# Two cross-attention and two feed-forward blocks on one core: low parts of the first weights and context tiles on DVE, statistics of x blocks 4 to 7 ahead of evacuations

## The reference

```
x = x + _L0_xattn_ref(_layernorm(x), ctx_4096, Wq, Wk, Wv, Wo)      # 16 heads of 96, 4 key-value heads; keys: context and x itself
x = x + _L0_ffn_ref(_layernorm(x), ...)                             # relu(x up)^2 down, plus a routed low-rank part, layernorm
x = x + _L1_xattn_ref(_layernorm(x), ctx_4096, Wq, bq, Wkv, bkv, Wo, bo)   # 32 heads of 128, 8 key-value heads
x = x + _L1_ffn_ref(_layernorm(x), W, b, A, Bmat, LiMEs)            # x W + b, plus a gated low-rank part
```

## Time and profile before

| | before |
|---|---|
| median of 3 runs | 1207.34 us (1207.11 to 1208.05) |
| the profiled execution | 1206.82 us |
| its span | 1205.0 us |
| PE busy | 1159.5 us (96%) |
| DVE busy | 556.8 us (46%) |
| ACT busy | 506.0 us (42%) |
| POOL busy | 371.0 us (31%) |

### The profile page before, as it was taken

One profiled execution on the slowest core, in us unless ns is written; L12 is line 12 of the kernel. 1 busy time (PEld: TensorE's weight loads), 2 busy tenths in 40 slices (PEclk: granted clock), 3 DMA queues, 4 the chain that ended last, 5 costly groups with the idle time before them and its releaser, 6 DMA issues.

```text
span 1205.0 us, 15331 instructions
## 1 busy us (share of the span) xinstructions
PE 1159.5 (96%) x5582; PEld 916.4 (76%) x5582; DVE 556.8 (46%) x1011; ACT 506.0 (42%) x1377; POOL 371.0 (31%) x249
## 2 busy tenths in 40 slices
PE   5999999999999999996999999999999999999998
PEld 3777777777777768874888888888888888888774
DVE  4355346246237753258552533435243352433654
ACT  4365256247246624233452624435253351623620
POOL 3043034024024255455440502405032240412440
PEclk9999999999999999998999999999999999999997
DMA  7010001000000031200110100102001020100001
GB/s 255 1 40 27 1 26 39 0 26 26 0 18 1 1 117 58 88 35 1 36 53 1 52 35 35 52 0 87 1 35 52 2 85 0 38 35 1 12 1 70
DMA packets 10325, 43.42 MB, mean 36 GB/s; under 512 B 1301, under 2 KB 1557, under 8 KB 7605
## 3 DMA queue, kind: packets, MB, share of 16 engines
q1 hardware_dynamic: 10292, 42.99, 10.2%
HBM read 40.89 MB, written 2.10 MB: 36 GB/s over the span
## 4 chain that ended last, share of the span: by engine, by line
PE 85%; DVE 6%; ACT 4%; issue 3%; POOL 2%; DMA 0%; DVEq 0%; ACTq 0%; POOLq 0%
PE work L433 15%; PE work L435 15%; PE work L434 15%; PE work L494 7%; PE yb L433 5%; PE yb L435 4%; PE yb L434 4%; PE pt L504 3%; PE ov L435 3%; PE ov L433 3%; PE ov L434 3%; PE pt L435 3%; PE pt L434 3%; PE pt L433 3%; ACT prob L919 1%
## 5 line engine op out<-in xcount | busy, mean ns | idle before, releaser
L1089 POOL TENSOR_TENSOR prob<-prob,exp_rcp 128x512 f32<-128x512 f32 (+1 forms) x96 | 127.3, 1327 | 626.8 <-DVE exp_rcp L1264 626.8
L433 PE MATMUL work<-xT_hi,q_hi 128*128 128x512 f32 (+1 forms) x448 | 181.5, 405 | 4.8 <-DVE xT_lo L1349 4.8
L919 ACT ACTIVATE prob<-work,neg_max 128x128 f32<-128x128 f32 (+1 forms) x384 | 149.6, 408 | 74.4 <-DVE neg_max L1287 73.0
L435 PE MATMUL work<-xT_hi,q_lo 128*128 128x512 f32 (+1 forms) x448 | 177.8, 397 | 0.0
L434 PE MATMUL work<-xT_lo,q_hi 128*128 128x512 f32 (+1 forms) x448 | 177.7, 397 | 0.0
L494 PE MATMUL work<-kT,qT 128*128 128x128 f32 (+1 forms) x768 | 128.2, 310 | 1.1 <-DVE qT L1201 0.9
L494 PEld LDWEIGHTS work<-kT,qT 128*128 128x128 f32 (+1 forms) x768 | 114.1, 191 | 14.4 <-issue 1.7
L871 ACT ACTIVATE pT_hi<-pt 128x512 fp32r<-128x512 f32 x128 | 73.9, 603 | 109.1 <-PE pt L504 109.1
L1317 DVE TENSOR_TENSOR oT_lo<-ov,oT_hi 32x128 fp32r<-32x128 f32 (+2 forms) x160 | 67.3, 421 | 102.9 <-ACT oT_hi L877 101.6
L433 PE MATMUL yb<-o_hi,oT_hi 128*128 128x512 f32 x224 | 93.9, 419 | 10.4 <-DVE oT_lo L1317 10.4
L433 PEld LDWEIGHTS work<-xT_hi,q_hi 128*128 128x128 f32 (+1 forms) x448 | 81.4, 182 | 26.8 <-DVE xT_lo L1349 5.3
(11 more groups left out here) (182 smaller groups left out, 2109.1 us busy)
## 6 DMA issues: line engine op xcount, KB each, us to landing
q_raw<-in_l_q SPq DMA_DIRECT2D x8, 1024.0 KB, 4.7
o_raw<-in_l_o SPq DMA_DIRECT2D x8, 1024.0 KB, 4.7
kv_raw<-in_l_kv SPq DMA_DIRECT2D x8, 515.0 KB, 3.3
q_raw<-in_l_q SPq DMA_DIRECT2D x4, 768.0 KB, 4.3
o_raw<-in_l_o SPq DMA_DIRECT2D x4, 768.0 KB, 4.2
qT<-in_ctxT SPq DMA_DIRECT2D x4, 512.0 KB, 6.8
x<-in_x SPq DMA_DIRECT2D x2, 1024.0 KB, 12.1
q_raw<-in_up SPq DMA_DIRECT2D x2, 1024.0 KB, 6.3
```

Source lines behind the costliest of these rows:

```text
L433: pe.matmul(dst, l_hi, r_hi, start=first and k == 0, stop=False)
L435: mm = pe.matmul(dst, l_lo, r_hi, start=False, stop=last and k == n - 1)
L919: e = act.activation(prob[:, i % 2, g * L.keys:(g + 1) * L.keys], s[:, g, :], ACT.Exp, bias=neg_max[:, i % 2, g:g + 1], accum_out=exp_sum[ ...
L1089: pool.tensor_tensor(p, p, exp_rcp[:, b % 2, :].unsqueeze(2).broadcast_to([P, G, L.keys]), ALU.mult)\
```

## The change

Three things are moved, all in the first 60 us. kv_lo of the first head and cT_lo of k = 2 go from POOL to DVE, so that DVE makes kv_lo and then all four cT_lo, and PE has one semaphore fewer to wait for. On DVE the statistics and shifts of x blocks 4 to 7 go ahead of the evacuation of kv 1, the four norm_lo and the evacuation of kv 3. On ACT normalise_x of blocks 4, 5 and 6 each go ahead of norm_hi of 1, 2 and 3, and so ahead of the evacuations of kv 0 and kv 2; normalise_x of block 7 follows these. POOL's remaining order, PE's and SP's are as they were.

```diff
@@ tensor
-            pe.wait_ge(c_lo_pool, 1)
-            pe.wait_ge(c_lo_done, 3)
+            pe.wait_ge(c_lo_done, KT)
@@ scalar
-            for b in range(4):
-                norm_hi(N[0], b)
+            norm_hi(N[0], 0)
+            for b in range(4, 7):
+                normalise_x(N[0], b, x[:, b, :])
+                norm_hi(N[0], b - 3)
             evacuate(L0, S0, 0, *L0.ahead[0:4])
-            for b in range(4, NB):
-                normalise_x(N[0], b, x[:, b, :])
+            normalise_x(N[0], 7, x[:, 7, :])
@@ gpsimd
-            split_lo(kv_lo, kv_raw, kv_hi, 768, P, kv_hi_done, kv_lo_done, 0)
-            pool.wait_ge(c_hi_done, 3)
-            pool.tensor_tensor(cT_lo[:, 2, :], qT[:, 2, :], cT_hi[:, 2, :].bitcast(F32), ALU.subtract)\
-                .then_inc(c_lo_pool, 1)
@@ vector
-            for k in (0, 1, 3):
+            dve.wait_ge(kv_hi_done, 1)
+            dve.tensor_tensor(kv_lo[:, 0:768], kv_raw[:, 0:768], kv_hi[:, 0:768].bitcast(F32), ALU.subtract)\
+                .then_inc(kv_lo_done, 1)
+            for k in range(KT):
...
-            evacuate(L0, S0, 0, ("kv", 1))
-            for b in range(4):
-                norm_lo(N[0], b)
-            evacuate(L0, S0, 0, ("kv", 3))
             dve.wait_ge(x_loaded[1], 16)
             for b in range(4, NB):
                 statistics(N[0], x, b)
                 if b > 4:
                     shift(N[0], b - 1)
             shift(N[0], NB - 1)
+            evacuate(L0, S0, 0, ("kv", 1))
+            for b in range(4):
+                norm_lo(N[0], b)
+            evacuate(L0, S0, 0, ("kv", 3))
             norm_lo(N[0], 4)
```

More of the change, by code:

```diff
@@ L353, in build_program @@
         o_loaded, o_hi_done, o_lo_done = sem("o_loaded"), sem("o_hi_done"), sem("o_lo_done")
-        c_hi_done, c_lo_done, c_lo_pool = sem("c_hi_done"), sem("c_lo_done"), sem("c_lo_pool")
+        c_hi_done, c_lo_done = sem("c_hi_done"), sem("c_lo_done")
         out_stored = sem("out_stored")
```

## The result

| | before | after |
|---|---|---|
| median (11 runs each) | 1207.11 us (1204.45 to 1208.05) | 1209.81 us (1208.81 to 1210.16) |
| the profiled execution | 1206.82 us | 1209.81 us |
| its span | 1205.0 us | 1207.9 us |
| PE waits on xT_lo of block 3 | 1.41 us | 7.39 us |

The ratio is 1.0025, with an interval of 1.0016 to 1.0034: the changed kernel is slower by some 2.7 us.

A forecast was written before the change was run, and what follows sets the result against it. PE was taken to bound the kernel, with the start of kv 4 as the deciding point. +2.59 - 0.52 + 2.31 = +4.38 us on 1206.82 gave 1211.2, plus 0.52 for the median 1211.7; range 1209.2 to 1213.9.

The forecast's parts named there:

- What bounds, and where the loss is made: PE's waits in the first 60 us: only the start of kv 4 matters, forecast +2.59 us against 29.34.
- The early weights and context tiles: DVE makes kv_lo at 4.7; PE starts at about 9.1, 3.55 us earlier, and DVE's added work costs nothing.
- the 1 us kept for that in the range: SP's earlier kv_raw load might push x or q_raw back at most 1 us; taken as zero in the sum.
- The moved statistics: DVE stands before shift(4) until POOL ends q_lo at 25.22; PE resumes kv 4 at 31.93, +2.59 us.
- Block 4's wait: PE's 0.52 us wait before the transpose of block 4 goes, since that block is normalised by 27.
- The clock: PE idles 7.5 us before kv 4, then restarts at the lower clock, costing 2.31 us, zero as other end.
- I take the same 2.31: Clock price at kv 4, taken from twelve matmuls after a 4.82 us idle: 5.18 us against 2.87.
- the 0.52 that I added for the median over the profiled execution: Last step of the sum: the runs' median lies 0.52 us above the profiled execution, taking 1211.2 to 1211.7.
- Rival A, the clock holds: At PE's restart on kv 4: the same steps without the clock's 2.31 us, 1209.4; chance 5%.
- Rival B, POOL's first operation: POOL's first operation pays about 6 us wherever it stands, so rstd(0) begins at 21.6; 1217.5, chance 12%.
- Rival C, q_lo out of the way: POOL answers rstd(4) before q_lo, ACT decides, PE resumes at 27.3, 2.0 us earlier; 1204.8, chance 4%.

The follow-up runs named there:

- The doubled q_lo: The changed kernel with q_lo computed twice on POOL, in the same place: 1213.28 us, ratio 1.0047.
- the kernel with rstd first: The changed kernel with rstd of blocks 4 to 7 ahead of q_lo on POOL: 1208.98 us, ratio 1.0013.
- the filled pause: The changed kernel with extra products of 512 columns, never read, in PE's pause before kv 4: 1208.26 us with 7, 1213.19 us with 14.
- the small first operation: The kernel before with a one-number-per-partition operation on a constant put ahead of kv_lo on POOL: 1208.05 us in its one execution.

## Why the prediction came out as it did

**What bounds, and where the loss is made: right.** The start of kv 4 was the one point that mattered. The low tiles alone gained 4.2 us because that point moved with them, and in the changed kernel it moved the other way.

**The early weights and context tiles: right.** Kv_lo at 4.48 (4.7 predicted), PE's first product at 8.92 (9.1), the transpose of block 0 at 18.31 (18.3). That DVE would finish before x lands is shown by the 1.05 us that it still waits on the transfer. SP's load came at 10.56 instead of the 12.79 of the earlier trace rows, and x was no later for it (14.26 against 14.35 of the earlier trace rows): the 1 us kept for that in the range was not needed. From SP's timeline in the changed kernel:

```profile
10.56 0.35 SPq L379 DMA_DIRECT2D kv_raw<-in_l_kv  x1
```

**The moved statistics: right, step by step.** Shift(3) at 19.17 (19.25), q_lo from 21.64 to 25.12 (21.71 to 25.22), shift(4) at 25.66 (25.80), shift(7) at 28.57 (28.69), PE's restart at 31.82 (31.93). The doubled q_lo shows that this chain of waits is what sets the restart.

**Block 4's wait: right, slightly undersized.** It went, and the stretch from kv 4's start to that transpose shows its worth: 3.52 us in before (29.34 to 32.86) where kv 5 takes 2.88, so 0.64 and not the 0.52 of the row's bracket.

**The clock: the right mechanism, mis-sized.** The step that failed is "I take the same 2.31". The price in the changed kernel's trace was 4.14 less 2.88, so 1.26. I took one price, that of the earlier trace rows, as the price of a longer pause. The trace of before shows a second one 10 us ahead of it, which I passed over. PE's timeline there, and the busy time of 560 to 562:

```profile
559.03 0.66 PE L648 MATMUL pt<-ident,relu 128*128 128x128 f32 x4 [3.33 <-ACT relu L977]
```

```profile
560.00:562.00 2.00, 2.00 (x7) 1.57 (x6) 1.80 (x3) 0.55 (x1) 1.40 (x2) 0.56 0.00 0
```

Behind 3.33 us of idling the twelve products took 4.16 us from the first one's start to the last one's (559.44 to 563.60), where twelve like them shortly before took 2.64 (545.84 to 548.48): a price of 1.52. So before already gave a range, 1.5 to 2.3; the 1.26 lies a little below it.

By the changed kernel's trace the sum then is +2.48 - 0.64 + 1.26 = +3.10, and the scores moved by +3.05, where the prediction had +4.38. The other part of the 1.9 us is the 0.52 that I added for the median over the profiled execution; here the two are the same 1209.81.

What the price hangs on stays open. It is not the pause's length alone, as two comparisons show. At kv 4 it was 1.26 after 7.39 us, but 2.35 after 7.12 us in the kernel with rstd first, 2.27 after 3.89 us with q_lo behind the shifts, and 1.53 after 3.54 us with the statistics alone. And at the beginning of the second layer, where the program is the same in all kernels, the twelve products that took 5.18 us in before took 4.19 (573.54 to 577.73 in the kernel with the statistics alone, above) to 5.29 in the ten others. The pauses ahead of them differ too, 3.71 to 6.37 us, but after four nearly equal ones (4.81 to 4.83) they took 5.18, 5.09, 4.89 and 4.44. So one kernel's single trace gives one draw out of some 1.3 to 2.4 us. From the first scores to the end of the span, where nothing was changed, the traces took 1148.2 to 1150.1 us: a difference of one or two microseconds between two traces may be such draws and nothing else. The medians above are safer.

**Rival A, the clock holds: fell in the changed kernel** (0.50 from 32 to 34), and the filled pause shows that it would have held had PE been kept busy. Its 1209.4 is near the result all the same, because only 1.26 of the clock's 2.31 came and the 0.52 for the median did not; the time alone could not have told A from the forecast, and the trace does.

**Rival B, POOL's first operation: fell.** Rstd(0) began at 15.52, not at 21.6, 0.17 after its input. The rule that I cited beside it, in the Trainium skill, GPSIMD Engine Reference, section 2.1 Instruction dispatch, of about 6 us for the first call to a freshly loaded kernel without the wait for its event, taken as an addition to the first operation, is not what these runs show: the small first operation had its input 10.8 us before it started, and the changed kernel's had it 0.17 before.

**Rival C, q_lo out of the way: right that it would not happen here, wrong in its working.** Its 1204.8 was worked out from rstd(4) being answered ahead of q_lo. Done so, it gave 1208.98, since q_lo then ran beside the last shift and held it. Only once q_lo stood behind that shift too did PE resume at 27.27, as C had it (27.3), and the median came to 1205.09. That it lies so near 1204.8 is in part luck: C has no price for the clock, and kv 4 paid 2.27. In that trace the first scores start only 0.49 us earlier than in before (54.58); of the further 1.3 us in its span, 0.82 came in the second layer, where the twelve products of the earlier trace rows took 4.36 us instead of 5.18.

## What to carry to other kernels

When an instruction is moved ahead on one engine, read the other engine's queue at the new time: an operation that used to answer at once may now stand behind a long one that has nothing to do with it (here 4.32 us of waiting for an rstd of 0.55). A gain ahead of a joining point counts only if the last arrival at that point moves; take the two halves of a change apart before keeping either, as one may hide the other's gain. A price read off one event in one trace, as that of a clock drop, is a draw: look for every event of its kind in the trace, and put it into the sum as a range.

## What the runs showed of the chip

A DVE operation with two inputs in the large memory is held while POOL subtracts two tiles there, even one of a single number for each partition: 3.37 us for the shift begun just behind q_lo, 0.16 for the shift ahead of it, in two kernels that differ by that one wait. The trace of before already had it in another place, DVE's cT_lo of k = 3 beside POOL's kv_lo. The timelines of the two engines in before:

```profile
12.03 1.65 DVE L1355 TENSOR_TENSOR cT_lo<-qT,cT_hi 128x1024 fp32r<-128x1024 f32 x1 [1.68 <-ACT cT_hi L989]
```

```profile
10.79 1.80 POOL L1077 TENSOR_TENSOR kv_lo<-kv_raw,kv_hi 128x768 fp32r<-128x768 f32 x1 [9.97 <-issue]
```

In the changed kernel, with POOL idle, this cT_lo takes 1.23. Beside kv_lo it ended 1.09 us after kv_lo in each of three traces, however early it began: at 13.68 after 12.59 here, at 14.68 after 13.59 with the small operation first (2.62 us), at 14.96 after 13.87 with the statistics alone (1.35 us). Norm_lo, which reads one input from a bank of products, was not held: in the kernel with q_lo behind the shifts all four ran while POOL had q_lo, the first two in the 1.27 us that they take in the changed kernel, where q_lo was over. The timelines of DVE and POOL in it:

```profile
24.75 1.27 DVE L1346 TENSOR_TENSOR xT_lo<-pt,xT_hi 128x512 fp32r<-128x512 f32 x2
```

```profile
24.31 3.44 POOL L1077 TENSOR_TENSOR q_lo<-q_raw,q_hi 128x1536 fp32r<-128x1536 f32 x1 [0.27 <-DVE minus_mean L1334]
```

In these traces POOL does no tensor operation before about 11 us into the program (10.79, 11.64 and 12.03 in three kernels), also one whose input has been there since 0.8. Work for the first microseconds is better given to DVE, which began kv_lo at 4.48.

The lower clock's price differs from trace to trace, 1.3 to 2.4 us for the same twelve products. What decides it was not found.
